# Graph attention on one core: VectorE scales all three of its units before it copies the next quad's terms, and ScalarE makes the sloped scores after its last head

## The reference, cut to what matters

```python
h = jnp.maximum(_layernorm(x, axis=-1), 0.0)
# _L1_gnn_ref: 12 heads (H) of 64 (D)
ft = jnp.einsum('nhd,ed->nhe', hh, W_fc)
a1 = jnp.einsum('nhd,hd->nh', ft, attn_l)
a2 = jnp.einsum('nhd,hd->nh', ft, attn_r)
e = jax.nn.leaky_relu(a1[src] + a2[dst], negative_slope=0.2)
m = jax.ops.segment_max(e, dst, num_segments=n)
ee = jnp.exp(e - m[dst])
denom = jax.ops.segment_sum(ee, dst, num_segments=n)
alpha = ee / denom[dst]
agg = jax.ops.segment_sum(alpha[:, :, None] * ft[src], dst, num_segments=n)
res = jnp.einsum('nhd,ed->nhe', hh, W_res)
x = x + jax.nn.relu((res + agg).reshape(n, H * D))
```

## Time and profile before

| | us |
|---|---|
| median of 3 runs | 1934.32 (1932.88 to 1934.53) |
| span of the profiled execution | 2277.0 |
| attention stage in the profile | about 1560 to 2277 |

### The profile page before, as it was taken

How to read it: one execution, slowest core, us unless ns; L and a number is a source line. 1 busy time by engine, 2 the same in 40 slices (tenths; PEclk the granted TensorE clock), 3 DMA queues, 4 the chain that set the end, 5 groups by cost and what they waited for, 6 DMA issues and landing times. The chain is left out here.

```text
span 2277.0 us, 43588 instructions
## 1 busy us (share of the span) xinstructions
PE 1621.1 (71%) x13579; PEld 962.8 (42%) x13580; DVE 1121.9 (49%) x2027; ACT 718.1 (32%) x2184; POOL 1232.7 (54%) x1297
## 2 busy tenths in 40 slices
PE   7337888887778858787788887882666666666665
PEld 7223444444344424344444444671334444444443
DVE  6613334333334314444444444653666666666666
ACT  6400111111111101000000100262666666777675
POOL 2166566566656266566666666106555555555550
PEclk9969888899988869798988888986787777878877
DMA  4698888888878387788787887388788888888882
GB/s 183 218 315 269 268 266 271 274 265 277 275 264 270 125 279 270 261 270 277 262 274 266 266 275 274 122 310 280 245 279 267 270 267 272 273 273 272 273 276 84
DMA packets 139992, 585.22 MB, mean 257 GB/s; under 512 B 30616, under 2 KB 32752, under 8 KB 139946
## 3 DMA queue, kind: packets, MB, share of 16 engines
q0 software_dynamic: 100272, 497.49, 65.7%
q1 hardware_dynamic: 32563, 67.72, 8.6%
q10 hardware_dynamic: 7110, 19.43, 2.2%
HBM read 534.42 MB, written 50.12 MB: 257 GB/s over the span
## 5 line engine op out<-in xcount | busy, mean ns | idle before, releaser
L667 POOL DMA_INDIRECT ring_c<-table,slot_c x834 | 798.1, 957 | 545.9 <-issue 268.5
L1243 POOL DMA_INDIRECT ring<-table,slot x417 | 410.4, 984 | 288.5 <-issue 105.8
L833 DVE TENSOR_TENSOR hots<-iota,units 128x256 f32<-128x256 bf16 x102 | 43.3, 426 | 602.4 <-remote 332.9
L1493 PE MATMUL ps_acc<-ring,hot_f 128*32 128x195 f32 x3136 | 230.8, 386 | 138.2 <-issue 84.4
L1388 ACT ACTIVATE ring<-ring,weight x1152 | 281.5, 340 | 0.6
L1651 DVE TENSOR_TENSOR ring<-ring,ps_w 128x3120 f32 x72 | 244.7, 3398 | 16.5 <-issue 8.9
L1493 PEld LDWEIGHTS ps_acc<-ring,hot_f 128*32 128x32 f32 x3136 | 123.9, 125 | 227.7 <-issue 124.2
L808 PE MATMUL ps_ya<-weights,sum_ta 128*128 128x512 f32 (+1 forms) x576 | 204.1, 503 | 12.5 <-issue 10.9
L808 PE MATMUL ps_yb<-weights,sum_tb 128*128 128x512 f32 (+1 forms) x576 | 196.7, 494 | 6.1 <-issue 5.5
L711 ACT ACTIVATE slot_c<-units 128x8 int32 (+1 forms) x104 | 21.7, 211 | 545.9 <-DMA ring_c<-table,slot_c 391.8
L779 PE MATMUL ps_sum0b<-ring_c,hots 128*32 128x192 f32 x1600 | 136.3, 364 | 75.9 <-issue 66.6
(11 more groups left out here) (294 smaller groups left out, 2121.0 us busy)
## 6 DMA issues: line engine op xcount, KB each, us to landing
ring_c<-table,slot_c POOLq DMA_INDIRECT x834
table<-ft SPq DMA_DIRECT2D x25, 396.0 KB, 2.8
table<-nodes SPq DMA_DIRECT2D x25, 384.0 KB
table<-nodes ACTq DMA_DIRECT2D x25, 384.0 KB
turned_table<-h_t SPq DMA_DIRECT2D x25, 384.0 KB, 3.0
nodes<-in_x ACTq DMA_DIRECT2D x24, 384.0 KB
turned_g<-turned_table SPq DMA_DIRECT2D x24, 384.0 KB
out_x<-nodes SPq DMA_DIRECT2D x24, 384.0 KB
```

Source lines behind the costliest of these rows:

```text
L667: eng.indirect_dma_start(out=ring[:, t * QH + k, :], out_offset=None, in_=table, in_offset=bass.IndirectOffsetOnAxis(ap=slot[t][:, k:k + 1 ...
L833: eng.tensor_tensor(hots[k][:, :, :].rearrange("p (s c) d -> p s c d", c=CPU), iota0[:, :].unsqueeze(1).unsqueeze(2).to_broadcast([P, 2, C ...
L1243: eng.indirect_dma_start(out=ring[:, b * RB + at * FROW:b * RB + (at + 1) * FROW], out_offset=None, in_=table3, in_offset=bass.IndirectOff ...
L1493: last = eng.matmul(acc_of(s, g), hot_f[:, c, s * UD:(s + 1) * UD], ring[:, x0 + g * GW:x0 + (g + 1) * GW], start=False, stop=True, skip_g ...
```

## The change

```diff
             def early_of(j):
-                return min(2, units_of(j) - 1)
+                return min(3, units_of(j) - 1)
...
                                 for h in range(H):
                                     head = rows[:, c * FROW + h * FH:c * FROW + (h + 1) * FH]
                                     last = eng.activation(head, head, ACT.Copy, scale=weight[:, c, h:h + 1])
-                                if c == CPU - 2:
-                                    sloped(q + 1)
                             last.then_inc(scaled[mine], 1)
+                            sloped(q + 1)
                             if has_before(j):
                                 with eng.If(nth < 1):
                                     lay(j - 1)
```

## The result

The changed kernel takes **1900.53 us** (1898.04 to 1901.22, 4 runs) against 1934.42 us before: ratio 0.9826, 95% interval 0.9812 to 0.9841, 33.9 us faster. The forecast was 1932 us, which is no change that a run could tell, in a range of 1905 to 1952.

What follows compares the result with a forecast made beforehand. Nearly continuous DMA transfers were taken to bound the attention: 23.4 us a quad plus about 0.9 us. Of at most 0.9 x 23 = 21 us it took 0.1 us a quad, 2 us: 1932 us, range 1905 to 1952.

Steps and rivals of the forecast that it cites:

- The queue: DMA queue as q+2's gathers begin: not empty in either order, so 0.1 us a quad gained, 2 us.
- the hole: First profile, ScalarE before L1344: 5.37 us wait for unit 3's products, holding the profile's extra 4.3 us a quad.
- Unit 2 ahead of the terms: VectorE: the 1.40 us wait goes; with late rows, everything behind the terms is 3.4 us shorter.
- Sloped behind all heads: ScalarE: heads end at 1732.8 instead of 1736.5; `lay` comes 2.9 us earlier to 0.7 us later.
- The unloaded quad redone: Last full quad in the new order: `lay` at 2242.7 against 2242.61, bare loop changed by 0.1 us, none.
- C: Attention quad: the chain through the landing, not DMA, is the wall; 53 us at most, 1898 us; chance 0.10.
- B: The 0.9 us gap above DMA time is the waits on VectorE and ScalarE that go; 1915 us; chance 0.25.
- D: Next scores come later and set the pace, 0 to 1.8 us a quad slower; 1948 us; chance 0.25.
- A: Attention quads: the gain stays hidden behind nearly continuous DMA transfers; 1932 us, own range 1926 to 1938; chance 0.40.

Runs made afterwards that it cites:

- experiment 12: The changed kernel with the transposed input tile loaded once for all tiles, 0.39 MB a quad less: 1902.74 us, 0.9843 of the kernel before.
- terms_and_sloped: Kernel before with VectorE's terms behind unit 2 and the sloped copy behind all heads, TensorE's order as before: 1897.41 us, 0.9808; again 1896.92 us, 0.9816.
- 13: terms_and_sloped with the transposed input tile loaded once for all tiles: 1899.59 us, 0.9825 of the kernel before.
- second profile: The kernel before, unchanged, run and profiled once more: 1932.77 us, ratio 1.000.
- terms_only: Kernel before with only VectorE's terms moved behind unit 2; TensorE's order and the sloped copy as before: 1931.97 us, 1.0004.
- terms_and_products: Kernel before with early_of = 3 on VectorE and TensorE, the sloped copy left among ScalarE's heads: 1965.85 us, 1.017.

## Why the prediction was wrong

**The step that failed** is the first one, "in the runs the transfers are nearly continuous, and a quad costs its 23.4 us of DMA plus about 0.9 us". Four things were wrong in it.

*The scale.* I carried a quad of 28.6 us to the runs by the ratio of the spans, 0.850, and got 24.3; measured is 23.75. And I took the DMA's busy time of that execution, 23.4 us, as its need. By the windows above it is 0.93 x 23.75 = 22.1 us before and 0.97 x 22.35 = 21.7 after, at 333 / 0.93 = 358 and 349 / 0.97 = 360 GB/s of busy time, against 269 / 0.82 = 328 in the earlier trace rows. A wall of 23.4 us isn't there: the changed quad is shorter than it. The figure of the Trainium skill that I weighed lightly (DMA: Bandwidth & Descriptors, Specifications, about 358 GB/s) agrees with both.

*The wall itself.* The share of 0.96 that I worked out for the runs is close to the 0.93 found, but a high share doesn't make a bound: with 5% fewer bytes the changed kernel didn't move (experiment 12), nor did `terms_and_sloped` (13).

*The queue.* "The queue isn't empty at that point in either order" was the reason for taking 0.1 us a quad and not 0.9. It was empty in the very quad of the earlier trace rows, right after GpSimd had stood 3.1 us for the release of unit 0, to 1727.01:

```profile
1727.00:1728.00 1.00, 1.00 (x32) 0.74 (x24) 0.00 (x0) 1.00 (x6) 0.95 (x1) 1.00 0.00 0
```

The last numbers are the DMA share and GB/s, both 0. An earlier release doesn't only lengthen the queue, it starts the gathers earlier; in the profile that agrees with the runs the loop through them is the quad (23.6 us).

*The warning.* A recording 18% longer than the runs, with 84.4 us of "issue" ahead of the attention's products, was to be read as an execution of another kind. I named the hole and still scaled through it. In the second profile those products wait for VectorE's scaling and not for issue. The first profile (1590 to 2240 us), then the second (1400 to 1860 us):

```profile
L1493 PE MATMUL ps_acc<-ring,hot_f 128*32 128x195 f32 x2951 | 219.3, 385 | 123.3 <-issue 84.4 <-DVE ring L1651 34.6 <-ACT ring L1388 3.9
```

```profile
PE ps_acc L1493 <- DVE ring L1651: 77.3, 57, 3.3
```

The range has a slip of its own: 1 us a quad either way of 1934 us is 1911 to 1957, and the text says 1905 to 1952. The result is outside both.

**The part-by-part steps.** *Unit 2 ahead of the terms*: "everything behind them is 3.4 us shorter" is right in direction and too large: terms to maxima is 4.6 us now (1661.19 to 1665.74, held by ScalarE's copy) and was 6.1. Alone it is worth nothing (`terms_only`); beside the sloped copy's move it is worth nearly 18 us (1915.00 to 1897.41), by the traces mostly because `finish` comes earlier for `lay` (1.2 us of waiting a quad go), a wait that the prediction doesn't have. *Sloped behind all heads*: I had `lay` 2.9 us earlier to 0.7 us later; counted from the weights it is 0.6 us earlier in the two quads shown and 1.4 us on average, inside the bounds, and I priced it at nothing because of the wall. I took the scores as what the copy waits for; before the change it was VectorE's signal. *The unloaded quad redone*, from the earlier trace rows, put the sloped copy at 2242.0, 15.0 us after the weights: the changed kernel has 15.1 to 15.4 in 22 of its 24 quads. So the redone quad was the forecast to make. It says 22.0 us or a little more; 22.35 was measured. What it needed beside it was the loaded quad of before, which waits 2.7 us for rows and runs 1.8 us over its own bare loop of 21.9.

**The rivals.** C ("the chain through the landing is" the wall), with 0.10 and 1898 us, had the mechanism, and its chain from landed rows over the weights, the release and the gathers is the loop found. That its time came out is partly luck: the "two thirds" of the way to 22.0 us had no reason beside it. B's 1913 to 1915 us was the same direction with the wall kept. D's mechanism, scores pushed by unit 2's products and the later terms, is real: it is the whole of `terms_and_products`, +34 us; in the full change the 12 heads leave the tail at the same time and outweigh it, 2.9 to 1.4 us. So D's signs (the copy later than 13.6 us, L1344 right behind `lay`) were seen in a kernel that is faster. A, which I preferred, fell.

Still open: what held TensorE in the first recording and on one chip; what takes VectorE's stream 3.5 us from the terms to its signal; and whether TensorE's part of the change costs 3 us or nothing. The fastest order tried is `terms_and_sloped`, 0.9808 and 0.9816, not told apart from the change.

## What to carry to other kernels

When a recording is much longer than the runs, don't scale it: look for the idle time that has no releaser, and build the quad again from durations and order alone, as was done here for the unloaded quad. A busy DMA isn't a wall until fewer bytes are shown to help. On an in-order engine, put the instruction that waits for somebody behind all work that doesn't need it, and look at what the work behind it waits for in its turn: the sloped copy's move alone gave half, because `lay` then stood waiting for `finish`; `early_of` without it gave a loss as large as the gain. Where a buffer is two deep, follow the chain through the release and the next fill: a microsecond saved on it is worth half a microsecond a quad at most, and nothing more once the engines' own order is as long.

## What the runs showed of the hardware that was not expected

The same kernel took 1932 us on most chips used and 2290 us on one, where TensorE issued stretches of products one per 0.73 us, without a wait that the profile shows, and where neither 4 us less of ScalarE's work nor 5% fewer bytes a quad moved the time by more than about 0.2%. The DMA engines ran at a share of 0.97 and 349 GB/s, with a time that 5% fewer bytes left as it was. Before the change they stood at 0.93, and yet ran dry for about a microsecond at a time (a share of 0.08 from 1538 to 1539 us) when GpSimd waited for a part of the ring. From the start of a quad's last gather until VectorE, which waited for the rows, copied the terms it took 5.6 us on average (4.9 to 6.5).
